# The gate's bias in a one-layer language-model tower: from two matmuls per pair to one VectorE addition

## The reference

```
x = emb[inp]
q, k, v = x @ Wq.T + bq, x @ Wk.T + bk, x @ Wv.T + bv          # 16 heads of 16
h = softmax(q k^T / 4) v, heads joined, @ Wo.T + bo

n = layernorm(h)
Bu_proj = (n @ B_w.T) @ C_w.T
state = exclusive scan over the tokens of Bu_proj with decay = sigmoid(log_decay)
gate = sigmoid(n @ gate_w.T + gate_b)                           # gate_b: 256 numbers
h = h + gate * state
out = h + layernorm(h) @ sign(weight).T
```

## Time and profile before

| | before |
|---|---|
| median of three runs | 740.04 us (739.85 to 740.42) |
| the profiled execution's own time | 740.43 us |
| its span, first to last instruction | 738.7 us |
| PE busy | 690.1 us, 93% |
| PEld busy | 649.1 us, 88% |
| ACT busy | 577.4 us, 78% |
| DVE busy | 518.6 us, 70% |
| POOL busy | 376.9 us, 51% |
| mean granted TensorE clock | 0.977 of full speed |

### The profile page before, as it was taken

One profiled execution on the slowest core, in us unless ns is written; L12 is line 12 of the kernel. 1 busy time (PEld: TensorE's weight loads), 2 busy tenths in 40 slices (PEclk: granted clock), 3 DMA queues, 4 the chain that ended last, 5 costly groups with the idle time before them and its releaser, 6 DMA issues. The chain is left out here.

```text
span 738.7 us, 21201 instructions
## 1 busy us (share of the span) xinstructions
PE 690.1 (93%) x7047; PEld 649.1 (88%) x7047; DVE 518.6 (70%) x1147; ACT 577.4 (78%) x1643; POOL 376.9 (51%) x431
## 2 busy tenths in 40 slices
PE   4589999999999999999999999999999999999862
PEld 3478999999999999999999999999999999998762
DVE  3656777778777777777777777787777777877532
ACT  2488888888888888888888888888888888888510
POOL 7402354555556545455465555554555555544553
PEclk9799999999999999999999999999999999999986
DMA  5422233332223333332333333322233333221000
GB/s 142 112 91 90 97 115 104 113 112 93 81 87 101 114 111 102 113 102 69 89 95 114 114 99 114 104 77 86 87 114 114 99 114 106 87 82 69 16 15 28
DMA packets 56016, 69.68 MB, mean 94 GB/s; under 512 B 6768, under 2 KB 41648, under 8 KB 55984
## 3 DMA queue, kind: packets, MB, share of 16 engines
q1 hardware_dynamic: 52048, 60.48, 24.1%
q0 software_dynamic: 3072, 8.39, 6.7%
q10 hardware_dynamic: 864, 0.40, 0.2%
HBM read 10.52 MB, written 8.39 MB: 26 GB/s over the span
## 5 line engine op out<-in xcount | busy, mean ns | idle before, releaser
L372 ACT ACTIVATE probs<-ps_s,neg_max 128x128 f32<-128x128 f32 x1024 | 295.5, 383 | 74.9 <-DVE neg_max L518 74.9
L518 DVE TENSOR_REDUCE neg_max<-ps_s 128x4 f32<-128x512 f32 x256 | 175.9, 688 | 96.9 <-PE ps_s L641 93.8
L294 POOL TENSOR_TENSOR xn<-h,mv 128x512 f32<-128x512 f32 x64 | 66.7, 1042 | 216.5 <-DVE ve L545 216.5
L381 ACT COPY probsT<-ps_t 128x512 f32<-128x512 f32 x256 | 157.6, 615 | 15.0 <-PE ps_t L717 11.3
L717 PE MATMUL ps_t<-ident,probs 128*128 128x128 f32 x1024 | 154.3, 273 | 6.5 <-ACT probsT L381 6.2
L717 PEld LDWEIGHTS ps_t<-ident,probs 128*128 128x128 f32 x1024 | 119.9, 141 | 13.0 <-issue 5.1
L641 PE MATMUL ps_s<-k_stack,q_stack 128*128 128x256 f32 x512 | 123.7, 323 | 3.9 <-DMA q_stack<-q_low 3.9
L641 PEld LDWEIGHTS ps_s<-k_stack,q_stack 128*128 128x128 f32 x512 | 77.7, 192 | 4.3 <-DMA q_stack<-q_low 4.3
L287 POOL DMA_INDIRECT x_emb<-in_emb,id_col x64 | 64.8, 1013 | 23.2 <-issue 14.1
L307 POOL TENSOR_TENSOR state_high<-state_in,ones_col 128x512 fp32r<-128x512 f32 x32 | 33.2, 1037 | 81.3 <-DVE state_in L630 81.3
L533 DVE BATCH_NORM_STATS2 stats<-h 128x6 f32<-128x256 f32 x128 | 48.2, 418 | 33.9 <-POOL h L319 32.8
(11 more groups left out here) (126 smaller groups left out, 1877.3 us busy)
## 6 DMA issues: line engine op xcount, KB each, us to landing
k_stack<-k_high SPq DMA_DIRECT2D x128, 128.0 KB
q_stack<-q_high SPq DMA_DIRECT2D x64, 256.0 KB
k_stack<-k_low SPq DMA_DIRECT2D x64, 128.0 KB
q_stack<-q_low SPq DMA_DIRECT2D x32, 256.0 KB
out<-y SPq DMA_DIRECT2D x32, 256.0 KB, 2.1
x_emb<-in_emb,id_col POOLq DMA_INDIRECT x64, 3.8
raw<-in_wkT SPq DMA_DIRECT2D x1, 256.0 KB, 3.4
raw<-in_wqT SPq DMA_DIRECT2D x1, 256.0 KB, 4.5
```

What stands on the lines that cost most here:

```text
L294: nc.gpsimd.tensor_tensor(xn[:], h[:], mv[:, :, 0:1].to_broadcast([P, 2, D]), ALU.subtract).then_inc(centred, 1)
L372: last = nc.scalar.activation(probs[s % 2][:, j], ps_s[s % 2][:, j * SEQ:j * SEQ + SEQ], ACT.Exp, bias=neg_max[s % 2][:, j:j + 1])
L381: nc.scalar.copy(probsT[st][:], ps_t[:]).then_inc(act_pT, 1)
L518: nc.vector.tensor_reduce(neg_max[s % 2][:], ps_s[s % 2][:].rearrange("p (h k) -> p h k", h=HPS), axis=AX.X, op=ALU.max, negate=True).then ...
```

## The change

The matmuls of the bias and what they need (one_of_each, gb_high, gb_parts and the instructions that fill them) are gone. Instead DVE adds the bias row gb_row, which is loaded as the same row on all 128 partitions as before, to the bank g1 and writes the sum to a new SBUF tile gate_in. This stands between maxima(6) and ctxTl. It waits for the gate's matmuls (pe_gate) and for the tanh of the pair before (act_tanh), and signals dve_gate. ACT's tanh reads gate_in and waits for dve_gate, and the users of g1 on TensorE wait for dve_gate instead of act_tanh. The semaphore bias_made is renamed earlier_made.

```diff
-                nc.scalar.copy(gb_high[:], gb_row[:]).then_inc(act_prep, 1)
-                nc.scalar.copy(gb_parts[0:64], gb_row[0:64]).then_inc(act_prep, 1)
...
                 if exists(t - 2):
-                    await_event(act, pe_gate, 1, t - 2, 1)
+                    await_event(act, dve_gate, 1, t - 2, 1)
                     await_event(act, dve_gated, 1, t - 3, 1)
-                    nc.scalar.activation(gate_tanh[:], g1[:].rearrange("p (b d) -> p b d", b=2), ACT.Tanh,
-                                         scale=0.5).then_inc(act_tanh, 1)
+                    nc.scalar.activation(gate_tanh[:], gate_in[:], ACT.Tanh, scale=0.5).then_inc(act_tanh, 1)
...
-                dve.wait_ge(act_prep, 2)
-                nc.vector.memset(one_of_each[:].bitcast(fp32), 0.0).then_inc(bias_step, 1)
-                dve.wait_ge(bias_step, 1)
-                for row in (0, 64):
-                    nc.vector.memset(one_of_each[row:row + 1].bitcast(fp32), 1.0).then_inc(bias_step, 1)
-                nc.vector.tensor_tensor(gb_parts[64:P], gb_row[64:P], gb_high[64:P].bitcast(fp32),
-                                        ALU.subtract).then_inc(bias_step, 1)
...
                 maxima(6)
+                if exists(t - 2):
+                    await_event(dve, pe_gate, 1, t - 2, 1)
+                    await_event(dve, act_tanh, 1, t - 3, 1)
+                    nc.vector.tensor_tensor(gate_in[:], g1[:].rearrange("p (b d) -> p b d", b=2),
+                                            gb_row[:].unsqueeze(1).to_broadcast([P, 2, D]), ALU.add).then_inc(dve_gate, 1)
                 low_features(t - 1, ctxT, g2, act_ctxT, pe_o, dve_ctxlo)
...
-                    if bias is not None:
-                        terms.append((one_of_each[:], bias[:]))
...
                 if exists(t - 1):
-                    await_first((act_tanh, 1, t - 3, 1), (dve_klo, C, t, C))
+                    await_first((dve_gate, 1, t - 3, 1), (dve_klo, C, t, C))
                     context_rows(0, g1)
...
-                    await_first((dve_klo, C, t + 1, C), (dve_ctx, 2, t - 1, 1), (act_tanh, 1, t - 3, 1))
-                    token_major(g1, wg, xn1T, PARTS, pe_gate, gb_parts)
+                    await_first((dve_klo, C, t + 1, C), (dve_ctx, 2, t - 1, 1), (dve_gate, 1, t - 3, 1))
+                    token_major(g1, wg, xn1T, PARTS, pe_gate)
```

More of the change, by code:

```diff
@@ L81, in build @@
         ones_col = sb("ones_col", [P, 2])
-        gb_row, gb_high, gb_parts = sb("gb_row", [P, D]), sb("gb_high", [P, D], f32r), sb("gb_parts", [P, D], f32r)
-        one_of_each = sb("one_of_each", [P, SEQ], f32r)
+        gb_row = sb("gb_row", [P, D])
         zero_col = sb("zero_col", [P, 1])
@@ L117, in build @@
         xn1, xn2 = sb("xn1", [P, 2, D]), sb("xn2", [P, 2, D])
-        gate_tanh = sb("gate_tanh", [P, 2, D])
+        gate_in, gate_tanh = sb("gate_in", [P, 2, D]), sb("gate_tanh", [P, 2, D])
         state_in = sb("state_in", [P, 2, D])
@@ L144, in build @@
         exp_ld, act_prep, powers_made, powers_turned = sem("exp_ld"), sem("act_prep"), sem("powers_made"), sem("powers_turned")
-        bias_made, bias_step = sem("bias_made"), sem("bias_step")
+        earlier_made, dve_gate = sem("earlier_made"), sem("dve_gate")
         col_copied, rs1_done, rs2_done = sem("col_copied"), sem("rs1_done"), sem("rs2_done")
@@ L260, in _ @@
             nc.gpsimd.memset(neg_half[:], -0.5).then_inc(const_step, 1)
-            nc.gpsimd.memset(earlier_raw[:], 1.0).then_inc(bias_made, 1)
-            pool.wait_ge(bias_made, 1)
+            nc.gpsimd.memset(earlier_raw[:], 1.0).then_inc(earlier_made, 1)
+            pool.wait_ge(earlier_made, 1)
             nc.gpsimd.affine_select(out=earlier_raw[:], in_=earlier_raw[:], compare_op=ALU.is_ge, fill=0.0, base=-1,
-                                    pattern=[[1, SEQ]], channel_multiplier=-1).then_inc(bias_made, 1)
-            pool.wait_ge(bias_made, 2)
-            nc.gpsimd.tensor_copy(earlier[:], earlier_raw[:]).then_inc(bias_made, 1)
+                                    pattern=[[1, SEQ]], channel_multiplier=-1).then_inc(earlier_made, 1)
+            pool.wait_ge(earlier_made, 2)
+            nc.gpsimd.tensor_copy(earlier[:], earlier_raw[:]).then_inc(earlier_made, 1)
             nc.gpsimd.memset(ones_col[:], 1.0).then_inc(const_step, 1)
@@ L662, in await_prepared @@
                 pe.wait_ge(powers_made, 3)
-                pe.wait_ge(bias_made, 3)
-                pe.wait_ge(bias_step, 4)
-                pe.wait_ge(act_prep, 3)
+                pe.wait_ge(earlier_made, 3)
             PARTS = ((0, 0), (0, 1), (1, 0))
@@ L676, in feature_major, with token_major @@
                 last.then_inc(done, 1)
-            def token_major(dst, weight, src, parts, done, bias=None):
+            def token_major(dst, weight, src, parts, done):
                 for b in range(2):
```

## The result

| | before | after |
|---|---|---|
| median, us (lowest to highest, runs) | 740.42 (739.85 to 741.44, 5) | 735.12 (733.52 to 738.42, 5) |
| profiled execution, us (span) | 740.43 (738.7) | 738.42 (736.4) |
| ratio after/before | | 0.9932 [0.991, 0.9953] |

The changed kernel is faster by 5.3 us. 7.9 us were forecast, and 735.12 lies inside the range of 730.3 to 736.4. The profiled execution of after happens to be the slowest of its five, so what it lost on top must be told from what the change does in every execution.

A forecast was written before the change was run, and what follows sets the result against it. TensorE's queue was taken to set the pace in the steady part. Removed matmuls 7.14 + 0.34 + 0.42 = 7.9 us, nothing added elsewhere: 740.04 - 7.9 = 732.1, rounded up to 732.2 us; range 730.3 to 736.4.

The forecast's parts named there:

- both ends of the clock: Feed-forward at the end: earlier work may meet other clock stretches, plus or minus 0.9 us, taken as 0; 731.2 to 733.1.
- the xn1Tl rival: Steady turns: the gate waits for DVE's xn1Tl instead, so at most 0.1 us a turn is kept; 736.2 us, chance 0.13.
- The removed matmuls: TensorE, turns 2 to 31: 60 bias matmuls at a start spacing of 0.119 us, worth 7.14 us.
- The addition: DVE, after maximum 7: 680 ns a pair, hidden in idle time; 1.4 us of idle remain before maximum 8; cost nothing.
- The tanh: ACT: reads gate_in from SBUF instead of PSUM; no change in duration, and waiting for DVE costs nothing.
- Turn 32: First turn without attention: addition waits for the gate, ctxTl queues behind it, fits with 0.3 us to spare.
- The last gate, 0.42 us: Last turn, TensorE: the bias pair removed is worth 2 x 0.21 us, from 26 ps_g matmuls in 5.49 us.
- Worth between 0 and 0.2 us; I take 0: The start: DVE loses three memsets and a subtraction, ACT two copies; first scores wait for q_low's DMA until 27.82.
- the steady ones: Rivals in steady turns, including the gate waiting for xn1Tl (736.2 us, 0.13) and nothing won there (739.3 us, 0.05).
- The slower one: Steady turns: the addition pushes DVE's maximum 8, deciding below 0.6 us of idle time; some 750.8 us, chance 0.06.

The follow-up runs named there:

- old setup kept: Changed kernel, but ACT's two copies, DVE's three memsets and subtraction, and TensorE's two waits at the start stay in, though nothing reads the result: 733.43 us, 0.991.
- the addition alone: Kernel before with its bias matmuls kept, plus DVE's addition of a row of zeros between bank and tanh: 741.14 us, 1.0017.
- five additions: Changed kernel with DVE's old setup kept and four more additions of the same form ahead of gate_in in every turn: 761.2 us, 1.0275.
- only matmuls out: Kernel before without the two bias matmuls of each gate and without any addition, all of the setup kept: 732.95 us, 0.9911.
- the kernel with the spare DMA: Changed kernel with all the old setup, plus one spare 256 KB DMA ahead of the stack's last three transfers in turn 0: 733.69 us, 0.9891.
- the program that gave a packet at 36.8 us: Changed kernel with DVE's three memsets, subtraction and two waits of the old setup back in: 733.0 us, then 734.95 us when run again.
- the shifted code: Changed kernel with six small matmuls at the start of TensorE's program, which move all later code: 734.16 us, 0.9906.

## Why the prediction was right, and where it was off

The mechanism came as forecast, in the steady turns to the hundredth of a microsecond. The total is another matter. The forecast with both ends of the clock was 731.2 to 733.1, and 735.12 lies outside it. That it lies in the stated range is luck: the range goes up to 736.4 for the sake of the xn1Tl rival, and that did not happen.

**The removed matmuls: right.** Sixty at 0.119 us were to shorten a turn by 0.24; the 14 turns behind the first gate became 3.30 us shorter, 0.235 each, in the kernel with the old setup kept, and the same within 0.02 us in both repeats of the changed one. Turns of 20.78 us were read where 20.8 stood.

**The addition: right.** 682 ns, hidden. DVE's idle time before maximum 8 is 1.77 us, more than the 1.4 forecast, because against maximum 7 ctxTl moved by 0.15 us and not by 0.3, and maximum 8 came 0.08 us sooner and not 0.24. Both experiments say the same: 0.5 us with the addition against without, and 1.0017 [0.9998, 1.0036] with nothing else changed.

**The tanh: duration off, effect right.** "No change" was 57 ns short. The estimate by the Trainium skill ("VectorE: DVE Perf Modes", section on the TRN2 errata), 43 ns, was nearer. By that figure 1.4 us of ACT work arise, by the measured 57 ns 1.8. The 57 are a mean: in the last two turns, which have no attention, the tanh is 31 ns longer (about 630 instead of 600), and in the others it takes 653 to 771 where it took 622 to 627. What lengthens it there wasn't looked into. The copy probsT behind it still waits 0.21 us for TensorE (the earlier trace rows had 0.28), so it costs nothing. The forecast left only 0.04 us there, because it moved TensorE's transposes and not ACT's own work; the tanh starts 0.27 us ahead of the transposes after, 0.26 before, so ACT moved with TensorE.

**Turn 32: right.** The addition waits for the gate, ctxTl follows. DVE's rows of after, and the matmul that needs it:

```profile
699.74 0.69 DVE L615 TENSOR_TENSOR gate_in<-ps_g,gb_row 128x512 f32<-128x512 f32 x1 [2.66 <-PE ps_g L634]
700.34 0.68 DVE L514 TENSOR_TENSOR ctxTl<-ps_g,ctxTh 128x512 fp32r<-128x512 f32 x1
```

```profile
701.43 0.37 PE L634 MATMUL ps_g<-woh,ctxTh 128*128 128x256 f32 x1
```

0.4 us to spare, 0.3 forecast.

**The last gate, 0.42 us: not in this execution.** The chain that ended last (start us, us, what), which answers to the earlier trace rows:

```profile
711.38 5.49 PE ps_g L634 x24
...
718.78 1.23 PE ps_g L634 x8
...
730.99 2.09 PE ps_g L634 x8
```

24 matmuls took the 5.49 us that 26 took before. In the other kernels without the bias matmuls the same 24 took 4.38 to 5.49. This term is the clock's to give, and the plus or minus 0.9 us of the prediction covers it.

**The step that failed** is "Worth between 0 and 0.2 us; I take 0", on the start. It asked only whether the removed setup work lay on the path to the first scores. It did not ask what is exposed between those first scores and the first gate: there TensorE waited for ACT's probsT six times in the kernel before (4.6 us from 26 to 60 us), the stack's last transfer came just in time for 46.07 (in after 2.84 us passed from its issue at 45.05 to the scores; from 43.40 the same makes 46.24, an estimate), and a stretch of low clock followed where it came late. The profiled execution of after lost 2.8 us there (51.3 us from the first scores to the first gate, 48.5 before), and 1.1 to another late transfer at 170 us, at full clock.

How much of it belongs to the change? At 48 us no gate has run yet (the first stands at 75 us or later), so neither a removed matmul nor an addition can have caused that wait by its own time; only the shorter setup, the place of the code, or chance can. Pooled, the changed kernel took 734.97 us (20 runs, 732.06 to 738.53) and the kernel before, beside the experiments, 740.52 (42 runs, 737.99 to 744.9): 5.5 us. Each run also has its mean granted clock. At 0.975 or below were 7 of the 42 runs of before, 4 of 12 with the addition alone, and 35 of 66 of all kernels without the bias matmuls (five additions left out). Among the runs at 0.976 or above the medians are 740.37 and 733.01 us: 7.4 apart, nearly the 7.9 of the sum. Among the others 744.29 and 735.09. So the missing time goes with a lower clock, which about half the executions without the bias matmuls have, and one in six did before. That is an association and no proof: the runs were sorted after the fact, by a quantity that itself goes with the time, and the mean takes in the start and the end as well. It isn't the late packet alone either: of the seven profiles with one, five are at 0.975 or below and two at 0.977, of the six without, none.

Why it is so often now isn't settled. No single part of the setup brings the time back in runs of its own. The setup as a whole isn't ruled out: the two kernels that keep all of it (only matmuls out, old setup kept) took 733.02 us pooled (11 runs), 2.0 less than the changed one; the kernel with the spare DMA, which keeps it too, took 733.69. Nor are TensorE's two waits: with them the packet came early in 5 of 6 profiles, without them late in 7 of 8, but the medians, 733.43 (23 runs) and 734.49 (43 runs), are only 1.1 us apart. And the program that gave a packet at 36.8 us gave one at 43.6 in the next profile, so chance has a part in any case. Enough profiles of one kernel with and without the two waits, or a kernel that keeps the bias matmuls in the first turns only, would tell; neither was made.

**The rivals.** None of the steady ones happened: no wait for xn1Tl, no wait of each turn. The slower one has its point of decision elsewhere than was written, at ctxTl with 1.57 us.

## What to carry to other kernels

In a queue that sets the pace, count an instruction at the spacing of starts and not at its duration, and look for the next engine's room at the place where the pacing engine will want the result of what is pushed back, not at the next idle gap. Read the first turns apart from the steady ones: there transfers arrive just in time, a wait of 1 us can cost as much again or more in clock (1.2 and about 1.7 us here), and executions of one program differ by 3 to 6 us. When a gain of 1% comes out a third short, compare stretch by stretch across several profiled executions before a part of the change is blamed.

## What the runs showed of the hardware that was not expected

- A packet of 16 KB of code among the stack's transfers goes with an SP issue that takes longer by 0.8 to 1.3 us (2.52 for two instead of 1.27; 2.08 when it fell one transfer earlier), and all transfers queued behind it start that much later. At the place before the wait at 48 us this is so in all eight profiles with a late packet.
- In the seven profiles whose wait at this place was 0.65 to 2.15 us the granted clock fell to 1.2 GHz during the wait or as it ended; with the wait of 0.46 us it didn't. The length of a wait alone doesn't decide it: behind 1.06 us at 170 us in after, 1.31 at 168 with the shifted code, and 0.93 to 0.98 at 58 to 64 us in all 14 profiles the clock stayed at 2.4 GHz. At 48 us TensorE had also been less busy ahead of the wait: 1.49 of the 3.8 us from 44.0 on in after, 2.44 before.
- A tanh of 128x512 from SBUF: 680 ns on average, from PSUM 623; in the last two turns, which have no attention, about 630 and 600.
